# Local attention layers: values weighted into transposed outputs, probabilities divided ahead of it, and the mask written by ScalarE

## The reference, cut to the local layers

```python
def local_attention(q, k, v):                 # b, 16 heads, n = 256, d = 64
    bq = q.reshape(b, h, nw, w, d)            # nw = 8 windows of w = 32
    bk2, bv2 = look(bk), look(bv)             # the window before and the own one: 64 keys
    mask = (it < jb) | (it > jb + w) | (jb == -1)
    sim = jnp.einsum('bhwie,bhwje->bhwij', bq, bk2) * 8.0
    sim = jnp.where(mask, -jnp.finfo(sim.dtype).max, sim)
    attn = jax.nn.softmax(sim, -1)
    out = jnp.einsum('bhwij,bhwje->bhwie', attn, bv2)
    return out.reshape(b, h, n, d)

for i in range(6):
    x = attn_layer(shift_tokens(x), Wqkv[i], q_scale[i], k_scale[i], Wo[i]) + x   # l2norm, rotary, local_attention, Wo
    x = ffn_layer(shift_tokens(x), ...) + x   # layer norm, W1, a * gelu(gate), W2
```

## Time and profile before

| | |
|---|---|
| Three runs, us | 3877.47, 3895.34, 3896.42; median 3895.34 |
| Profiled execution, us | 3887.87; its span 3886.1 |
| TensorE matmul busy over the span | 3293.4 us (85%) |
| TensorE weight loads | 2520.4 us (65%), beside the matmuls |
| VectorE | 2667.7 us (69%) |
| ScalarE | 1962.0 us (50%) |
| GpSimd | 1539.4 us (40%) |
| First and last projection of heads in the local layers | 568.1 and 2360.6 us |

### The profile page before, as it was taken

The page is one execution under the profiler, slowest core; times in us unless marked ns, Lnnn a source line. Parts: engine busy times, 40 slices in busy tenths (PEclk is TensorE's granted clock), DMA queues, the critical chain, the costliest instruction groups (busy, mean ns, idle before and its releaser), DMA issues. The chain is left out here.

```text
span 3886.1 us, 125922 instructions
## 1 busy us (share of the span) xinstructions
PE 3293.4 (85%) x54593; PEld 2520.4 (65%) x54593; DVE 2667.7 (69%) x4862; ACT 1962.0 (50%) x3747; POOL 1539.4 (40%) x1459
## 2 busy tenths in 40 slices
PE   6665949999999999999999998599999886866557
PEld 2223528888888888888888886467777775522235
DVE  6996457787787777778777775665556533699713
ACT  5452326666666666666666664244444442255323
POOL 1662025444544444444545441422222221066542
PEclk8997969999999999999999998687888876889878
DMA  1000011111101111101101100000000000000111
GB/s 43 1 1 19 0 41 50 38 30 42 41 27 44 38 28 46 38 27 46 40 25 29 30 27 11 7 6 7 7 7 7 7 5 7 8 1 1 65 59 46
DMA packets 72478, 96.94 MB, mean 25 GB/s; under 512 B 14678, under 2 KB 48244, under 8 KB 70788
## 3 DMA queue, kind: packets, MB, share of 16 engines
q1 hardware_dynamic: 69668, 84.74, 7.3%
q0 software_dynamic: 2272, 4.27, 0.3%
HBM read 35.60 MB, written 8.40 MB: 11 GB/s over the span
## 5 line engine op out<-in xcount | busy, mean ns | idle before, releaser
L2208 POOL TENSOR_TENSOR local_rot<-local_term 128x512 f32<-128x512 f32 x384 | 480.7, 1275 | 860.8 <-DVE local_term L2559 860.8
L2559 DVE TENSOR_TENSOR local_term<-bank,local_table 128x512 f32<-128x512 f32 x768 | 486.3, 683 | 114.5 <-ACT local_sq L2439 112.8
L278 POOL TENSOR_TENSOR mamba_hc<-mamba_state,mamba_c_all 128x512 f32<-128x512 f32 x256 | 326.2, 1296 | 256.0 <-DVE mamba_state L502 248.6
L2214 POOL TENSOR_TENSOR local_rot<-local_rot,local_inv 128x512 f32<-128x512 f32 x384 | 399.5, 1061 | 67.3 <-ACT local_inv L2450 45.8
L2237 PE MATMUL bank<-local_w_layer,local_xs 128*128 128x256 f32 x1536 | 367.2, 382 | 4.6 <-ACT local_xs L2433 3.7
L2237 PEld LDWEIGHTS bank<-local_w_layer,local_xs 128*128 128x128 f32 x1536 | 279.0, 192 | 36.1 <-ACT local_xs L2433 4.0
L502 DVE TENSOR_TENSOR_SCAN mamba_state<-bank,mamba_dbu 128x512 f32<-128x512 f32 x256 | 298.1, 1205 | 0.0
L425 ACT ACTIVATE bank<-mamba_dt,mamba_a_neg 128x510 f32<-128x510 f32 x256 | 176.4, 690 | 226.6 <-DVE mamba_state L502 223.0
L339 PE MATMUL bank<-mamba_hc,ident 128*128 128x512 f32 x512 | 263.6, 640 | 24.0 <-DVEq L511 18.3
L2471 ACT ACTIVATE local_attn<-bank 128x512 f32<-128x512 f32 x192 | 115.1, 599 | 299.9 <-PE bank L2312 299.9
L2439 ACT ACTIVATE local_sq<-bank 128x512 f32<-128x512 f32 x384 | 227.6, 593 | 59.5 <-PE bank L2237 59.5
(11 more groups left out here) (423 smaller groups left out, 7673.6 us busy)
## 6 DMA issues: line engine op xcount, KB each, us to landing
local_v_moved<-local_v_at SPq DMA_DIRECT2D x192, 198.0 KB, 2.5
local_w_layer<-a_w_layer_dram SPq DMA_DIRECT2D x6, 1536.0 KB, 7.1
local_v_moved<-local_v_at SPq DMA_DIRECT2D x192, 33.0 KB, 2.8
routed_w<-f_w_dram SPq DMA_DIRECT2D x3, 2048.0 KB, 17.9
local_w_o<-a_w_o_dram SPq DMA_DIRECT2D x6, 512.0 KB, 3.4
rows_dram<-fresh SPq DMA_DIRECT2D x1, 2574.0 KB, 11.9
routed_x_in<-rows_dram SPq DMA_DIRECT2D x13, 198.0 KB, 4.7
routed_y_in<-y_dram SPq DMA_DIRECT2D x8, 256.0 KB, 4.7
```

Source lines behind the costliest of these rows:

```text
L278: ins = pool.tensor_tensor(hc[:, n % 2, h, :], state[:, n % 2, h, :], c_all[:, n % 2, :], ALU.mult)
L2208: pool.tensor_tensor(rot[:, s % 2, :, f, :], here[:, :, f, :], there[:, :, 1 - f, :], ALU.add).then_inc(summed, 1)
L2214: pool.tensor_tensor(one, one, spread(inv[:, s % 2, heads], E), ALU.mult).then_inc(normalized, 1)
L2559: dve.tensor_tensor(term[:, which, b, :], g.bank[b][:, :], table[:, which, :, :].rearrange("p n c -> p (n c)"), ALU.mult).then_inc(roped, 1)
```

## The change

Five things move together.

1. **Weighting.** The values become the stationary operand (64 keys by 64 channels), the turned probabilities are streamed, 32 columns a pass. The output stands transposed in the lower halves of banks 6 and 7, one for each half of the keys' rows, as the output projection wants it. `turn_out`, `scale_out` and the column of ones fall away.
2. **Division.** VectorE sums the exponents of each row and takes the reciprocal (`invert_weight`, after the sums of the squares); GpSimd multiplies the probabilities by it in place (`normalize_probs`, behind `add_turned(s+2)`), ahead of their turn.
3. **Mask.** From slot 1 on, ScalarE copies the mask from SBUF into the score bank (`open_scores(s+1)`, right behind `exponents(s)`), and the mask matmul stays in slot 0 alone.
4. **Banks.** Queries are turned through bank 4, keys through the upper halves of banks 6 and 7, so that both are turned one after the other.
5. **Order.** The turn of the probabilities and the weighting come a slot later, as the lists show.

```diff
+        O_BANKS, K_BANKS = g.last_banks[:, :, 0:HALF], g.last_banks[:, :, HALF:]
...
@@ GpSimd
+            def normalize_probs(s):
+                pool.wait_ge(over_ready, s + 1)
+                rows = z[:, s % 2, :].rearrange("p (x k) -> p x k", k=2 * W)
+                pool.tensor_tensor(rows, rows, spread(over[:, s % 2, :], 2 * W), ALU.mult).then_inc(p_normed, 1)
...
             for s in range(SLOTS):
                 if s + 2 < SLOTS:
                     add_turned(s + 2)
+                normalize_probs(s)
...
@@ TensorE
             def score(s):
-                pe.wait_ge(z_ready, s + 1)
-                pe.matmul(S_BANK[:, :], ident_b[:, :], mask[:, :, :].rearrange("p x k -> p (x k)"),
-                          start=True, stop=True, skip_group_check=True)
+                if s:
+                    pe.wait_ge(opened, s)
+                else:
+                    pe.matmul(S_BANK[:, :], ident_b[:, :], mask[:, :, :].rearrange("p x k -> p (x k)"),
+                              start=True, stop=True, skip_group_check=True)
...
             def turn_probs(s):
-                pe.wait_ge(e_ready, s + 1)
+                pe.wait_ge(p_normed, s + 1)
...
             def weigh_values(s):
-                pe.wait_ge(pt_copied, s + 4)
+                pe.wait_ge(pt_copied, s + 1)
                 pe.wait_ge(v_shifted, s * 32 + 32)
-                pe.wait_ge(o_normed, 2 * s) if s else None
+                pe.wait_ge(o_copied, s) if s else None
+                pe.wait_ge(k_copied, min(s + 4, SLOTS + 1))
                 for k in range(TPG):
-                    for hh in range(H):
-                        column = (k % 2 * H + hh) * ROW
-                        for r in range(2):
-                            for v in range(2):
-                                keys, row = slice(2 * W * v, 2 * W * (v + 1)), H * W * v + W * r
-                                mm = pe.matmul(g.bank[6 + k // 2][row:row + W, column:column + E + 1],
-                                               pt[keys, k, r, W * hh:W * (hh + 1)],
-                                               (v_at if r else v_moved)[keys, TPG * (s % BUFS) + k, hh, 0:E + 1],
-                                               start=True, stop=True, skip_group_check=True)
-                    if k % 2:
-                        mm.then_inc(o_ready, 1)
+                    for r in range(2):
+                        for v in range(2):
+                            for hh in range(H):
+                                keys, column = slice(2 * W * v, 2 * W * (v + 1)), (2 * k + r) * W
+                                mm = pe.matmul(O_BANKS[E * hh:E * (hh + 1), v, column:column + W],
+                                               (v_at if r else v_moved)[keys, TPG * (s % BUFS) + k, hh, 0:E],
+                                               pt[keys, k, r, W * hh:W * (hh + 1)], start=True, stop=True, skip_group_check=True)
+                mm.then_inc(o_ready, 1)
...
@@ ScalarE
+            def open_scores(s):
+                act.wait_ge(z_ready, s + 1)
+                act.activation(S_BANK[:, :], mask[:, :, :].rearrange("p x k -> p (x k)"), ACT.Copy).then_inc(opened, 1)
...
                 if s >= 2:
                     copy_out(s - 2)
+                exponents(s)
+                if s + 1 < SLOTS:
+                    open_scores(s + 1)
                 if s + 2 < SLOTS:
                     square(s + 2, 0)
-                exponents(s)
-                if s + 2 < SLOTS:
                     square(s + 2, 1)
...
@@ VectorE
+            def invert_weight(s):
+                dve.wait_ge(e_ready, s + 1)
+                own.step(dve.tensor_reduce(weight[:, :], z[:, s % 2, :].rearrange("p (x k) -> p x k", k=2 * W), AX.X, ALU.add))
+                dve.wait_ge(p_normed, s - 1) if s >= 2 else None
+                dve.reciprocal(over[:, s % 2, :], weight[:, :]).then_inc(over_ready, 1)
...
-                if s:
-                    scale_out(s - 1)
+                invert_weight(s)
```

More of the change, by code:

```diff
@@ L2071, in local_stack @@
         sums_q, logs_q, inv = sb("sums_q", [P, TPG * 4]), sb("logs_q", [P, TPG * 4]), sb("inv", [P, 2, TPG * 4])
-        most, over = sb("most", [P, 2, 2 * TPG]), sb("over", [P, H * TPG])
-        o_scaled = sb("o_scaled", [P, H * TPG, E])
+        most, weight, over = sb("most", [P, 2, 2 * TPG]), sb("weight", [P, 2 * TPG]), sb("over", [P, 2, 2 * TPG])
         pt = sb("pt", [P, TPG, 2, H * W])
@@ L2424, in _ @@
             act.wait_ge(made, 1)
-            for free, n in ((pt_copied, 3), (q_copied, 1), (k_copied, 1), (squared, 2), (act_ln, 1)):
+            for free, n in ((q_copied, 1), (k_copied, 1), (squared, 2), (act_ln, 1)):
                 act.sem_inc(free, n)
@@ L2626, in beside @@
                     copy_up(f, UP_AT[k - 1, "late"])
-            def scale_out(s):
-                for half in range(2):
-                    blocks = slice(TPG * half, TPG * (half + 1))
-                    src = g.bank[6 + half][:, 0:TPG * ROW].rearrange("p (x c) -> p x c", c=ROW)
-                    dve.wait_ge(o_ready, 2 * s + half + 1)
-                    own.step(dve.reciprocal(over[:, blocks], src[:, :, E]))
-                    dve.tensor_tensor(o_scaled[:, blocks, :], src[:, :, 0:E], spread(over[:, blocks], E), ALU.mult).then_inc(o_normed, 1)
+            def invert_weight(s):
[3 more added lines that the diff above has]
+                dve.reciprocal(over[:, s % 2, :], weight[:, :]).then_inc(over_ready, 1)
             make_table(0)
```

62 lines of the change are left out of this document (28 added, 34 removed).

## The result

The changed kernel takes 3967.27 us (median of four runs, 3957.57 to 3968.8), against 3895.88 for the kernel before: 1.9% slower, ratio 1.0193, 95% interval 1.0168 to 1.0217. The forecast was 3923 us, so the direction was right and the size was not: 79 us more than the profiled run before, where 35 were summed. The two profiled runs differ almost wholly in the local layers: from the first row maximum to the last it is 1789.6 us before and 1874.0 after, 84.4 more; the rest of the kernel took 3.5 us less.

A forecast was written before the change was run, and what follows sets the result against it. TensorE bounds the kernel now; after the change, a VectorE-ScalarE loop. Eight slots take 77.1 us against 75.77, 31 us over 23 times, plus 3 and 1: 35 us on 3887.9 gives 3923 us, range 3872 to 3985.

The forecast's parts named there:

- VectorE's loop: Local layers' bare slots: VectorE waits for exponents, mask copy and square in a row; 7.58 us a slot against 7.17.
- GpSimd's division: Bare slots: one more 128x512 product on GpSimd, 1.02 us, claimed hidden under the 7.58 us slot by 0.25 us.
- rival C: Local layers: GpSimd's chain binds, bare slots growing 0.2 to 0.4 us (3963 us), or TensorE's clock falls; chance 0.08.
- k = 0 and 3 to 7: Six of eight slots with feed-forward work: 45.48 us of slots plus up-projection copies, layer norm and a wait, 52.3 us.
- k = 1: Slot with output and down projections, the latter waiting for VectorE's residual: 15.8 us, bounds 15.4 to 16.1.
- k = 2: Slot with ScalarE's values and residual copies, then TensorE's transposes and scores: 9.0 us, bounds 8.65 to 9.2.
- 7.17 - 0.21 - 0.49: TensorE's bare slot less the mask matmul and the turn of outputs, put at some 6.4 us.
- 8.05 against 7.45: Layer norm's wait: ScalarE's deviation ready at 8.05 us, VectorE arriving at 7.45, put at 0.65 us.
- the term for the weighting: TensorE's 64 weighting passes a slot, taken at 0.9 us, between 0.55 and 1.1.
- The second term: TensorE's granted clock, taken as 1.00; a fall was to count only below 0.84, where 6.4 us exceeds 7.58.

The follow-up runs named there:

- E5: Changed kernel with the mask put back to a TensorE matmul ahead of the scores and ScalarE's mask copy removed: 3913.8 us, ratio 1.007 to the kernel before.
- E4: Changed kernel, weighting behind the heads' projection; ScalarE order first square, exponents, second square, mask copy, copy of outputs: 3879.5 us, ratio 0.997 to the kernel before.
- E1: Changed kernel with the weighting behind the heads' projection and ScalarE's copy of outputs behind both squares: 4011.5 us, ratio 1.031 to the kernel before.
- E6: As E1, but slots with the output projection keep the changed kernel's order on TensorE and ScalarE: 3933.8 us, ratio 1.010 to the kernel before.
- E8: Changed kernel with 32 unused transposes ahead of the first slot, shifting TensorE's later code by 64 instructions: 3973.0 us in one run.
- E10: E6 plus 14 unused transposes in each k = 2 slot, filling TensorE's wait for ScalarE's residual copy: 3935.8 us, ratio 1.012 to the kernel before.

## Why the prediction was wrong

Its mechanism held, step by step, wherever no stall fell and the clock held. **VectorE's loop** was right in each piece: the mask copy is 0.52 us to the next start, the wait 1.70, the slot 7.52; E5 and E4 shortened it from two ends. **GpSimd's division** takes 1.04 us and is hidden in bare slots, so rival C's first half fell. The six places k = 0 and 3 to 7 sum to 51.9 us (52.3), k = 1 takes 15.6 (15.8), k = 2 9.2 (9.0): 76.7 against 77.1. Two slips in the sums change nothing: 7.17 - 0.21 - 0.49 is 6.47 and not 6.4, and 8.05 against 7.45 is 0.60 and not 0.65.

**The step that failed is the term for the weighting.** It was sized as work, 0.9 us with bounds of 0.55 and 1.1, and that size was right: unstalled, its 64 passes go 15.0 ns apart ((966.89 - 966.05) / 56), 0.96 us. But the change also put it right behind the scores, so that 256 loads and matmuls stand in one row of 2.2 us, and the sum gave that new order no price. 32 times TensorE stood there for 0.2 to 2.1 us, mostly over 1 (44 us in all); the heads, the squares and VectorE came later by it. E1, E6 and E8 show it: without the row no stall; with it in k = 1 alone, stalls there alone; with the code shifted, other slots. That TensorE stands there for its next packet of instructions is shown by the packets' ends, 1.23 to 1.62 us ahead of each of the stands' ends. The kernel before had such stands too (17, 10 us), in scores that follow weighting, turn and mask; the prediction does not draw on that row of the waits view.

**The second term is the clock, put at 1.00.** Rival C counted it as a mean: a fall would matter only once 6.4 us at a lower clock exceeded 7.58, at 0.84. Measured is 0.97, and it costs, because the slow stretch comes right behind an idle time of TensorE, on the heads or the scores that the loop waits for: 1.7 of the 3.3 us in the slot shown. Nor does it need a stall: the sum for k = 2 has TensorE wait some 2 us for ScalarE's copies, and it did, 1.85 us at each second turn of the residual; what stands behind that wait was summed at full clock. k = 2 and 3 hold 1.27 of the 2.7 us, with three of the stalls, all in k = 3. Shares by run: of the 2.7 us by which eight slots exceeded the commonest, E6 took back 1.3 and E10 another 0.7; the rest are mainly k = 1 stalls left in E10 (0.4) and k = 2 in the new order (0.15).

That 3967 us still lies in the stated range of 3872 to 3985 is luck. The bounds of the sum ended at 3956; what lay above was there for rival C, whose first half did not come and whose second was priced otherwise.

The Trainium skill's TensorEngine Tiling (Array Packing) (Instruction Overhead) says that a matmul with one streamed column has the same latency as one with 60, and advises against tiling a dimension that is already small; the 65 columns streamed before lie just above its 60. The trace agrees on the size of the weighting's work: half the streamed columns, 32 instead of 65, gained nothing, 14.3 ns a pass before and 15.0 after; a latency of 60 cycles is not shown by these rows, which are rates over several tiles. Perfetto Trace Analysis (Identifying the Most-Contended Engine), also of the Trainium skill, would have the engine with the highest occupancy optimized first, and judges TensorE's headroom by its useful arithmetic and the share of its weight loads, not by its matmuls' busy share. The loads' share was 84% before (1453.89 of 1721 us), VectorE's 77%, so TensorE comes first by it. Here the trace speaks against it: TensorE had less to do, and the kernel took longer.

## What to carry to other kernels

Price an order as well as the work: when small loads and matmuls are put into one long row, look in the waits view for stands put down to "issue" in the rows that there are, and put long-running matmuls between two such rows, as E1 and E6 did with the heads (eight passes in 1.9 us). A stand of TensorE, or a wait of like length, costs its length and can then cost the slow clock behind it, on whatever comes next; so look at who waits for that, not at the mean clock. And before a copy is moved, ask for every reader of it, as E1 shows.

## What the hardware showed that was not expected

- TensorE stands up to 2.1 us inside or right behind a row of 128 small passes, at a place given by the count of instructions ahead of it, until 1.23 to 1.62 us after the end of a packet of 256 instructions (16384 bytes). In the 32 cases it went on 2.3 to 4.0 us after the row's first pass had started.
- A stand of 1.54 us was followed by a granted clock of 0.66; behind a wait of 1.85 us it fell at once, later, or not at all (E6's k = 2 slots of 9.37 us); a wait of 0.81 us, in the k = 0 slot shown, left it at 1.00, as the timeline of this turn and the stretch's row of busy times show (kernel after):

```profile
1041.87 0.65 PE L2294 MATMUL bank<-ident,local_z 128*128 128x128 f32 x4 [0.81 <-POOL local_z L2219]
```

```profile
1041.80:1044.30 2.50, 2.43 (x20) 2.26 (x20) 2.50 (x5) 1.87 (x4) 0.11 (x2) 1.00 0.00 0
```

- A mask copy of ScalarE from SBUF into PSUM, 128x512, takes 0.58 us, like its copies the other way (0.60 for the turned probabilities).
